# A cross-attention convolution and a quantized feed-forward layer: eight slots summed by four transposes, with VectorE adding half of the pairs

## The reference

```python
kv = einsum('bhil,bhjl->bijhl', k, v)           # 8 x 8 products of channels of a head
y = causal convolution of kv with ssm_kernel[h] along l     # by FFT in the reference
out = y + kv * D[h]
out = einsum('bijhl,bhil->bjhl', out, q)        # weighted by q = layernorm(x), summed over i
x = x + out
h = layernorm(x)
x = x + ((silu(h @ Wg) * (h @ Wu)) @ Wd)        # W = (int - 128) * scale, 256 -> 704 -> 256
```

## Time and profile before

| | us |
|---|---|
| median of 3 runs | 89.25 (89.08 to 89.4) |
| the profiled execution | 89.5 |
| its span | 87.3 |
| PE busy | 74.9 (86%) |
| VectorE (DVE) busy | 65.9 (75%) |
| GpSimd (POOL) busy | 52.4 (60%) |
| ScalarE (ACT) busy | 46.5 (53%) |

### The profile page before, as it was taken

The page is one execution under the profiler, slowest core; times in us unless marked ns, Lnnn a source line. Parts: engine busy times, 40 slices in busy tenths (PEclk is TensorE's granted clock), DMA queues, the critical chain, the costliest instruction groups (busy, mean ns, idle before and its releaser), DMA issues.

```text
span 87.3 us, 1537 instructions
## 1 busy us (share of the span) xinstructions
PE 74.9 (86%) x517; PEld 62.3 (71%) x517; DVE 65.9 (75%) x175; ACT 46.5 (53%) x115; POOL 52.4 (60%) x71
## 2 busy tenths in 40 slices
PE   5934846899999997999999899899999999998720
PEld 3622533698878665988888789787999989987610
DVE  0346999989999999097998798698977494479460
ACT  0503462549577459453779367573334695757400
POOL 5510799086299998989556319378344596247230
PEclk9999999999999999999999999999999999999996
DMA  1499249999998000000000000001200003001103
GB/s 30 149 235 351 104 123 255 385 387 368 327 296 269 7 0 0 0 0 4 0 11 0 0 0 0 0 12 48 68 0 0 0 0 128 0 0 60 60 0 120
DMA packets 7287, 8.28 MB, mean 95 GB/s; under 512 B 976, under 2 KB 6384, under 8 KB 7280
## 3 DMA queue, kind: packets, MB, share of 16 engines
q1 hardware_dynamic: 6784, 7.90, 28.5%
q10 hardware_dynamic: 432, 0.27, 1.0%
q0 software_dynamic: 64, 0.02, 0.1%
HBM read 7.12 MB, written 1.07 MB: 94 GB/s over the span
## 4 chain that ended last, share of the span: by engine, by line
PE 43%; DVE 38%; DMA 6%; ACT 4%; issue 3%; SPq 1%; POOL 1%
PE gate_up L902 12%; PE down L918 8%; PE turn L865 8%; DVE terms L651 6%; DMA toeplitz<-taps 6%; DVE terms L654 5%; PE conv L884 4%; DVE shift_f L632 4%; PE conv L886 3%; PE conv L885 3%; DVE hidden L666 3%; PE conv L902 3%; DVE shift_q L609 3%; DVE stats_q L596 2%; DVE terms L658 2%
## 5 line engine op out<-in xcount | busy, mean ns | idle before, releaser
L902 PE MATMUL gate_up<-f_parts,wgu 128*128 128x256 f16 x144 | 19.1, 273 | 0.3 <-DVE hidden L666 0.3
L305 POOL TENSOR_TENSOR products<-k_ext 128x512 f32<-128x512 f32 x14 | 17.8, 1284 | 0.0
L224 POOL TENSOR_TENSOR h_lo<-hidden,h_hi 128x256 fp32r<-128x256 f32 x18 | 13.0, 731 | 6.5 <-ACT h_hi L446 6.4
L902 PEld LDWEIGHTS gate_up<-f_parts,wgu 128*128 128x128 f16 x144 | 13.4, 98 | 2.5 <-DVE hidden L666 0.5
L441 ACT ACTIVATE gate_act<-gate_up,sg_sb 128x256 f32<-128x256 f32 (+1 forms) x20 | 9.4, 471 | 9.6 <-PE gate_up L902 9.3
L865 PE MATMUL turn<-ident,terms 128*128 128x128 f32 x108 | 13.1, 273 | 0.2 <-DVE f_parts L637 0.2
L884 PE MATMUL conv<-products,toeplitz 128*128 128x288 f32 x32 | 10.8, 419 | 2.8 <-DVE toeplitz L581 1.4
L865 PEld LDWEIGHTS turn<-ident,terms 128*128 128x128 f32 x108 | 12.1, 141 | 1.2 <-issue 0.4
L918 PE MATMUL down<-wd,h_hi 128*128 128x256 f32 x40 | 11.7, 318 | 0.4 <-DVE ffn_out L676 0.3
L651 DVE TENSOR_TENSOR terms<-conv,q_ext 128x512 f32<-128x512 f32 x16 | 10.9, 684 | 0.7 <-PE conv L886 0.6
L666 DVE SCALAR_TENSOR_TENSOR hidden<-gate_up,su_sb,gate_act 128x256 f32<-128x256 f32 (+1 forms) x20 | 9.5, 481 | 2.0 <-ACT gate_act L441 1.9
(11 more groups left out here) (57 smaller groups left out, 125.4 us busy)
## 6 DMA issues: line engine op xcount, KB each, us to landing
toeplitz<-taps_pad SPq DMA_DIRECT2D x3, 512.0 KB, 8.3
k_ext<-ctx_ext SPq DMA_DIRECT2D x3, 384.0 KB, 6.5
out<-x_sb SPq DMA_DIRECT2D x8, 128.0 KB, 1.7
wg_int<-wg_t SPq DMA_DIRECT2D x1, 704.0 KB, 6.2
wu_int<-wu_t SPq DMA_DIRECT2D x1, 704.0 KB, 7.6
wd_int<-wd_t SPq DMA_DIRECT2D x1, 640.0 KB, 7.9
x_sb<-x SPq DMA_DIRECT2D x1, 512.0 KB, 8.5
x_sb<-x ACTq DMA_DIRECT2D x2, 128.0 KB, 4.2
```

What stands on the lines that cost most here:

```text
L224: eng.tensor_tensor(low_of(i, t), hidden[up_lanes(t), i % 2, t, :], high_of(i, t), ALU.subtract).then_inc(done, 1)
L305: nc.gpsimd.tensor_tensor(view(products[:, n:n + 1], GROUP, [[MADE, HALVES], [GROUP, 4], [1, GROUP]]), view(k, 0, [[EXT * B, HALVES], [0, ...
L902: done = nc.tensor.matmul(bank_of(i, t)[:, n, :], wgu[:, c, column:column + P], f_parts[:, i % 2, part, c, :], start=(c == 0 and part == 0 ...
```

## The change

UNMERGED becomes 2, so tile 2 is merged too. A new `merge_back` on VectorE adds, for tiles 2 to 7, the back slots in pairs (1+2, 3+d4); it waits for the terms and for `wrap`. `sum_terms` then sums four slots and waits for both merges. The load of x tile 1 moves from ACT's queue to SP's, and the lists of all engines are permuted. GpSimd has one merge more; nothing else is added.

```diff
-UNMERGED = 3
+UNMERGED = 2
-SUMMED_SLOTS = [0, 2 * P, BACK, BACK + P + SPARE, BACK + 2 * (P + SPARE), CROSS]
+SUMMED_SLOTS = [0, 2 * P, BACK, BACK + 2 * (P + SPARE)]
+        def merge_back(eng, t):
+            z = terms[:, t % 2, :]
+            even = view(z, BACK, [[TERMS, HALVES], [2 * (P + SPARE), 2], [1, P]])
+            odd = view(z, BACK + P + SPARE, [[TERMS, HALVES], [2 * (P + SPARE), 2], [1, P]])
+            wait(eng, terms_ready, TILE_HEADS * (t + 1))
+            wait(eng, wrapped, t + 1)
+            eng.tensor_tensor(even, even, odd, ALU.add).then_inc(back_merged, 1)
 # sum_terms, for t >= UNMERGED
                     wait(pe, merged, t + 1 - UNMERGED)
+                    wait(pe, back_merged, t + 1 - UNMERGED)
 # SP's list of loads: k(0,1), direct(0,1), k(1,2), direct(1,2), then
+            load_x(1, 2, x_loaded[1])
 # ACT's list
-            act.dma_start(x_sb[:, 1, :], x[P:2 * P, :]).then_inc(x_loaded[1], 16)
```

More of the change, by code:

```diff
@@ L341, in _ @@
             pairs(4)
+            root_q(2)
             pairs(5)
@@ L344, in _ @@
             pairs(6)
+            pairs(7)
             root_f(0)
-            pairs(7)
             root_q(4)
+            merge(2)
+            root_f(1)
             pool.wait_ge(k_loaded[4], 16)
             pairs(8)
-            root_f(1)
             root_q(5)
@@ L491, in _ @@
             squares(9)
+            wrap(2)
+            norm_q(4)
+            evict_q(3)
             squares(10)
-            high_f(0)
-            wrap(2)
+            evict_q(4)
             squares(11)
-            norm_q(4)
+            norm_f(0)
             act.wait_ge(k_loaded[5], 16)
@@ L499, in _ @@
             squares(13)
+            squares(14)
+            convert_down()
+            high_f(0)
+            norm_f(1)
             norm_q(5)
-            norm_f(1)
-            evict_q(4)
             wrap(3)
-            squares(14)
             high_f(1)
-            convert_down()
-            squares(15)
             norm_q(6)
@@ L687, in _ @@
             direct(0)
-            moments_of_q(0)
             variance_of_q(0)
+            dve.wait_ge(k_loaded[1], 16)
+            all_products(1)
+            dve.wait_ge(x_loaded[1], 16)
+            stats_of_q(1)
+            shift_of_q(0)
+            moments_of_q(1)
+            variance_of_q(1)
             dve.wait_ge(direct_loaded[1], 16)
             direct(1)
-            dve.wait_ge(x_loaded[1], 16)
-            stats_of_q(1)
-            moments_of_q(1)
-            shift_of_q(0)
-            dve.wait_ge(k_loaded[1], 16)
-            all_products(1)
-            variance_of_q(1)
+            shift_of_q(1)
+            dve.wait_ge(taps_loaded, 32)
+            add_skip_to_taps()
             dve.wait_ge(direct_loaded[2], 16)
             direct(2)
-            dve.wait_ge(taps_loaded, 32)
-            add_skip_to_taps()
+            multiply_terms(0)
+            direct(3)
+            multiply_terms(1)
             dve.wait_ge(x_loaded[2], 16)
@@ L705, in _ @@
             moments_of_q(2)
-            shift_of_q(1)
+            stats_of_q(3)
             variance_of_q(2)
-            multiply_terms(0)
-            direct(3)
-            shift_of_q(2)
-            multiply_terms(1)
-            stats_of_q(3)
-            multiply_terms(2)
             moments_of_q(3)
             variance_of_q(3)
+            multiply_terms(2)
+            shift_of_q(2)
             multiply_terms(3)
@@ L1012, in _ @@
             downs(3, 0)
+            gates(3, 5)
             downs(3, 1)
-            gates(3, 5)
             downs(3, 2)
```

276 lines of the change are left out of this document (141 added, 135 removed).

## The result

The changed kernel takes 86.19 us (median of 4 runs, 85.25 to 87.23), before it 89.33 (89.08 to 89.65). Timed again beside another set of runs of before it is 85.6 against 89.51, 0.9554 [0.952, 0.9589].

A forecast was written before the change was run, and what follows sets the result against it. PE was taken as the bound, with VectorE also full to 33 us. Convolve(12) at 45.5, 36.3 of list and 2.6 idle gave 84.4 against 83.15; 1.3 onto 89.5, less 0.25 over the median: 90.5 us, range 87.5 to 92.4.

The forecast's parts named there:

- the 2.0 us of idle PE before the sum of tile 4: PE before sum_terms(4): merge_back(3) and (4) wait for GpSimd, so the sum can't start before 43.5.
- the price of the new order: All engines' lists: beyond the transposes saved, the rest of PE's list is only permuted, costed at nothing.
- What PE saves: PE's sums of tiles 2 to 7: fewer transposes save 3.1 us, of which 2.2 after the first gates.
- The adds: Six merge_back on VectorE: 0.60 to 1.85 us each, the high end being a wait for GpSimd.
- The start: Later load of x tile 1 queues VectorE behind GpSimd's pairs; multiply_terms(4) at 21.6 instead of 20.58.
- From the gates to convolve(12): Blocked VectorE operations delay the sum of tile 4; convolve(12) comes at 45.5 against 44.58 before.
- From convolve(12) to the end: PE's remaining list of 36.3 us plus idle time ends at 84.4 against 83.15, 1.2 us later.
- "The same idle time": PE from convolve(12) to the end: the 2.6 us idle inferred for before is charged again.
- The PE-bound gain: Rival, 0.29: VectorE's free time from 33 to 57 us pays for the adds, PE's saving arrives; 87.7 us.
- GpSimd blocked as well: Rival, 0.17: each merge_back also delays GpSimd's pairs and low through the SBUF lock; 91.7 us.
- The start that doesn't queue: Rival, 0.10: shift_q(1) passes before pairs(2), multiply_terms(4) is on time, 1.2 us regained; 89.3 us.

The follow-up runs named there:

- the kernel with the new start and the old tail: Changed order up to the first gates, then the order of before with adds of tiles 4 to 7 placed by hand; 91.52 us, 1.0278.
- the six-slot kernel: Changed kernel's lists without the six merge_back, six slots summed for tiles 2 to 7; 88.32 us, 0.9832.
- the kernel with the moved root: Changed start and old tail, with root_f(3) on GpSimd directly behind pairs(12) instead of pairs(14); 89.0 us, 1.0013.

## Why the prediction was wrong

The forecast had the direction wrong. Its mechanism exists, an add of VectorE that waits for a whole operation of GpSimd and holds PE up, but in the changed kernel it hardly occurs. Two terms failed: the 2.0 us of idle PE before the sum of tile 4, of which 0.21 came, and the price of the new order, put at nothing, which is worth 1.9 us behind the gates. By its steps:

- **What PE saves.** Right: 2.2 us behind the gates forecast, 2.2 measured with the adds left out. 80 transposes, as forecast.
- **The adds.** 0.60 to 1.85 us each and a mean above 1.0 forecast; they took 0.68 to 1.16, mean 0.87. The upper bound is real (1.76 in the kernel with the new start and the old tail), but in the changed kernel no merge_back waits for a whole 128x512 operation of GpSimd; the longest, 1.16 us, waits for most of a 128x256 one of 0.73.
- **The start.** shift_of_q(1) waits for pairs(2), as forecast. add_skip_to_taps does not wait for the next: it starts at 9.86 and takes 0.14 us, passing before pairs(3) gets hold. So direct(2) waits for pairs(3), to 11.30, not for pairs(4), to 12.4. The gate weights are converted from 18.23 (19.3 forecast) and multiply_terms(4) starts at 20.47 (21.6, where the terms of the forecast's own sum add up to 21.5). The first gates start 1.1 us earlier than forecast, as much as that.
- **From the gates to convolve(12): the step that failed.** The forecast put merge_back(3) at 35.4 behind pairs(11), multiply_terms(9) at 37.1 and the sum of tile 4 at 43.5 after 2.0 us of idle PE. VectorE was there at 34.16, while GpSimd had its root: 0.68 us, multiply 9 at 34.85, the sum at 39.97 with 0.21 us idle. shift_of_q(7), costed at 1.2 us, took 0.15. Of the 4.7 us by which PE's end was missed (84.4 forecast, 79.44 + 0.24 come), 3.5 had arisen by convolve(12): 1.1 at the gates and 2.4 from there. The error was to charge each blocked operation one after another in a walk that was already 1.2 us late: whether an add of VectorE costs 0.68 or 1.76 us hangs on which of GpSimd's operations it meets, and a walk with an error of 1 us cannot tell that.
- **From convolve(12) to the end.** "The same idle time" of 2.6 us over its list was charged; 37.7 us were taken for a list of 36.3, so 1.4. The 2.6 was not idle time, either: in the trace of before PE idles 1.54 us from 44.58 to 83.15, so about 1.0 is a list priced too low; in the changed kernel it idles 0.69 and works 37.03, the same as before. The forecast took the rest of the lists for a permutation without a price. The order is worth 1.9 us behind the gates (the six-slot kernel), more than the 1.1 that the adds cost.
- **The rivals.** The PE-bound gain was the one that came, with its own sign (less than 0.3 us idle before the sum of tile 4), and with 85.3 to 85.6 us it went 2 us beyond its 87.7, about what the order, which it too had given nothing, is worth. GpSimd blocked as well: the mechanism is there, its price was not. The start that doesn't queue: half right, and shown to decide nothing.

The SBUF lock works in the second direction as well, which no row of before shows. In the changed kernel pairs(11) starts while merge_back(3) runs and takes 1.47 us, pairs(12) 1.27; a root of GpSimd takes 1.01 us at 45.86, beside a merge_back, 1.00 at 6.24, beside all_products(1), and 0.54 to 0.59 elsewhere; with the old order a merge took 1.65 us. The Trainium skill (SBUF — State Buffer, Who interferes with whom) states this, and these numbers agree. In the other direction one measurement differs from what it says of operations that read SBUF: merge_back(3) beside GpSimd's root takes 0.68 us, so the root does not hold it up. What GpSimd's waits cost PE was not measured by itself; it is within the 1.1 us of the adds. GpSimd was idle 8.3 us from 33 to 57 before and is 4.1 now.

## What to carry to other kernels

Work moved from a full engine to one with free time pays if the order lets it fall into that time: the shorter sums with their adds made the new order 2.8% faster (0.9554 for 0.9832) and the old order, with the adds placed by hand, 1.3% slower. When a diff reorders hand-written lists, give the order a price of its own, by the idle time between named steps that it may remove, instead of nothing. Where VectorE has several operations with two SBUF inputs in a row and the first is blocked, look at the third: a short operation of GpSimd (a root) in its way took 1.1 us off it.

## What the runs showed of the hardware that I had not expected

- When a 128x1 operation of VectorE has been blocked, the two-input operation right behind it passes before GpSimd's next one gets hold, though GpSimd has no pause: 16x1 in 0.14 us at 9.86, 128x1 in 0.15 us at 38.03. Its size did not matter: an add of 128x512 passes as well, in the kernel with the moved root and three others of the old tail, and there GpSimd's next operation takes 1.25 to 1.26 us instead of 0.73. VectorE, then GpSimd of that kernel:

```profile
52.13 1.23 DVE L641 SCALAR_TENSOR_TENSOR shift_f<-moments_f,rstd_f 128x1 f32<-128x1 f32 x1 [0.28 <-POOL rstd_f L310]
53.28 0.68 DVE L234 TENSOR_TENSOR terms<-terms 128x512 f32<-128x512 f32 x1
53.99 0.84 DVE L225 TENSOR_TENSOR h_tail<-hidden,h_tail 64x256 fp32r<-64x256 f32 x1
```

```profile
52.06 1.28 POOL L325 TENSOR_TENSOR terms<-terms 128x512 f32<-128x512 f32 x1
53.30 1.25 POOL L225 TENSOR_TENSOR h_lo<-hidden,h_hi 128x256 fp32r<-128x256 f32 x1
```

  The next one in the row waits for GpSimd again: 1.37 us for 128x128 at 9.93, 1.76 for the add at tile 4, 0.84 for the subtraction above. And behind a blocked operation of 128x128 even a 128x1 does not pass. In the kernel before, against the three pairs of the earlier trace rows:

```profile
12.26 0.83 DVE L581 SCALAR_TENSOR_TENSOR toeplitz<-anti,skip_all,toeplitz 128x128 f32<-128x128 f32 x1
13.02 1.22 DVE L609 SCALAR_TENSOR_TENSOR shift_q<-moments_q,rstd_q 128x1 f32<-128x1 f32 x1
```

  Whether merge_back(4) placed right behind the blocked shift would pass was not tried.
- PE's clock can fall to half shortly behind a stretch with little work on PE. Windows of the first profiled execution of the changed kernel; the last three numbers of a line are the clock, the DMA share and GB/s:

```profile
11.00:13.00 2.00, 0.42 (x2) 0.19 (x2) 2.00 (x5) 1.48 (x7) 1.79 (x2) 1.00 0.06 14
13.00:15.00 2.00, 1.93 (x7) 1.42 (x8) 1.97 (x7) 0.52 (x2) 0.00 (x0) 0.81 0.87 220
15.00:17.00 2.00, 2.00 (x6) 1.43 (x5) 1.97 (x8) 0.12 (x1) 1.56 (x2) 0.50 0.97 332
17.00:19.00 2.00, 2.00 (x15) 1.68 (x14) 1.30 (x3) 0.95 (x2) 2.00 (x4) 0.84 1.01 390
```

PE had been busy 0.42 of the 2 us from 11 to 13. The clock is then at its lower level, 1.2 GHz, in 15 to 17 us, and the span is 1.6 us longer than in the execution at the full clock (85.3, 83.7). The six-slot kernel's profiled execution fell at the same place (0.50 from 15 to 17 us, PE busy 0.54 of 2 us from 11 to 13). In that without the adds the clock stayed full there and fell behind the second idle time (0.50 from 27 to 29 us, PE busy 0.83 of 2 us from 25 to 27). The idle time of 1.64 us at 11 also stands in the execution without a fall, with 0.36 of 2 us busy, so it is not enough by itself. With this start and tile 2 merged, 12 of 35 timed executions took over 1.5% longer than the fastest of their kernel, with this start and tile 2 unmerged, where PE idles 0.73 us ahead of turn_q(4) and not 1.69, 0 of 40. What decides stays open.
